# A graph network on one core: a first stage written out as one pipeline, and skip features added by TensorE

## Chip, core and metric

The kernel runs on one NeuronCore of a Trainium2 chip. The metric is the device time of one execution in microseconds (us), the median of several runs. Engines are named as in the profile: PE (TensorE), DVE (VectorE), ACT (ScalarE), POOL (GpSimd) and SP (SyncE, which here only issues DMAs).

## What is computed

6250 nodes with 128 features, 200000 edges sorted by destination. Two blocks, each with a residual. The change lies in the first block and in what prepares the edge lists; this is the part of the reference that it touches:

```python
h = jnp.maximum(_layernorm(x, axis=-1), 0.0)
# inside the first block
hn = _layer_norm(h, ln1_w, ln1_b)
h_skip = hn
ft = (hn @ W_att).reshape(n, H, DH)          # H = 10, DH = 13
...                                          # attention over the edges of each node, agg
out = jax.nn.elu(agg)
out = out.reshape(n, H * DH) @ hr_w + hr_b
out = out + h_skip
out = _layer_norm(out, in_w, in_b)
skip2 = out
out = jax.nn.elu(out @ w1 + b1)
out = jax.nn.elu(out @ w2 + b2)
return out + skip2
```

The second block is four graph convolutions over the same edges, done as dense products with a 6272 x 6272 matrix of edge counts.

## The kernel before, in words

Nodes are tiled by 128: 49 tiles, handled in 7 batches (`NB`) of 7 tiles (`BATCH`, 896 rows, `BW`). Edges are padded to 196 groups (`NG`) of 1024 (`GE`). The program is a row of stages with a barrier of all engines between them: `prelude` (the first stage), `attention`, `normalise`, `general_attention` (skipped for regular inputs), `node_update`, `convolutions`.

`prelude` does two unlike things. One is the node features (`node_features`): for each batch two layer norms (of x, rectified; then of that, with weight and bias), a transpose on PE, the projection by `W_att`, and two writes to DRAM, `hn_dram` (the normed features, needed again in the node update) and `ft_tab` (the projected ones, gathered by attention). DVE makes both norms' statistics and the whole second norm: four passes of 128x896, for mean (L570), scale (L577), weight (L582) and bias (L585). ACT makes the rectified first norm (L598) and copies the projection out (L611). A batch is a loop body, every buffer is single.

The other is the edge lists. The inputs `dst` and `src` are copied to padded lists in DRAM (L286 to L295), and when all fills are out (`pads_out`) the lists are read back in several layouts (L302 to L313): by partition of 1600 and of 1568 edges, the same shifted by one (`nxt_s`, to find where the order falls), and by group (`by_group`, 98 partitions). From them come: the counting (L368 on DVE compares every 56th destination with 1569 thresholds, L460 on PE sums that over partitions, 28 steps, with four buffers of `below` between them), the start of each strip of edges, the keys (L373 to L378, six passes), written to DRAM as `edge_key`, the sources turned by PE into `src_all` (L389), the group rows (`row_tab`), and the schedule. At the end POOL fetches keys by indirect DMA in 13 blocks (`BLOCKS`, four buffers, L272), PE turns each block (L490), DVE makes `key_cols` of it (L433) and ACT `low_cols` (L446), with one bank of PSUM between them. On every engine the node features stand first in the queue, then the counting, then keys, sources and rows, then the 13 blocks.

`node_update` is written out by hand as a pipeline over the 7 batches: in step i PE, ACT and DVE work on batches i-1, i and i+1. For batch i+1, PE turns the attention's output and projects it by `hr_w` in two parts (L1675, L1676: two matmuls for each of 7 tiles, each split in two by the fp32 type), DVE adds the normed features `hn`, loaded from DRAM, to the PSUM result (`add_skip`, L1517 and L1519), makes statistics, ACT normalises in place in `o` (L1603), DVE applies weight and bias (L1534, L1537) to give `s2`, PE turns `s2` for the feed-forward, and POOL adds `s2` to x (L1464).

Of the kernel before, what the change touches and what calls it, by code (L numbers as in the profile page):

```python
# [11 lines left out]
ds = bass.ds  # L12
# [58 lines left out]
def gnn_program(nc, t):  # L71
# [12 lines left out]
    hn_dram = dram("hn_dram", (NP, D), F32)  # L84

    top = ExitStack()
    with top:
# [25 lines left out]
        def ln_batch(nm, on):  # L113
# [7 lines left out]
                 agg_tab=agg_tab, edge_score=edge_score, adj=adj, hn_dram=hn_dram,  # L121
# [32 lines left out]
def rounds(engine, n, body):  # L154

    body(0, True)
    with engine.Fori(1, n) as i:
        body(i, False)


# [13 lines left out]
def prelude(nc, t, sb, pb, sem, g, ln_batch):  # L174

    dst_pad, src_pad, edge_key, ft_tab, row_tab, agg_tab = (g[k] for k in (
        "dst_pad", "src_pad", "edge_key", "ft_tab", "row_tab", "agg_tab"))
    x_sb, ident, ident_bf, ones, eps, irr_part, src_all, sched, shared, spots, key_cols, low_cols = (
        g[k] for k in ("x_sb", "ident", "ident_bf", "ones", "eps", "irr_part", "src_all", "sched", "shared", "spots",
                       "key_cols", "low_cols"))  # L180
    with ExitStack() as c:
        fill_no = sb("fill_no", [16, 512], I32, c)
        fill_zero = sb("fill_zero", [16, 512], I32, c)
        fill_neg = sb("fill_neg", [1, FRONT], I32, c)
        zero_f = sb("zero_f", [P, TAB // P // 5 * WA], F32, c)
        dst_p = sb("dst_p", [P, EXJ], I32, c)
        src_p = sb("src_p", [P, EXJ], I32, c)
        dst_s = sb("dst_s", [P, EJ], I32, c)
        strip_of = sb("strip_of", [P, EXJ], I32, c)
        keys = sb("keys", [P, EXJ, 2], F32, c)  # L190
        hi = key_cols[:].rearrange("p n a c -> p (n a c)")[:, 0:EXJ].bitcast(I32)
        kf = low_cols[:].rearrange("p n a c -> p (n a c)")[:, 0:EXJ]
        coarse = sb("coarse", [P, EJ // COARSE], F32, c)
        nxt_s = sb("nxt_s", [P, EJ], I32, c)
        falls = sb("falls", [P, EJ], F32, c)
        by_group = sb("by_group", [GH, 2, GE], I32, c)
        of_group_f = sb("of_group_f", [GH, 2, GE], F32, c)
# [19 lines left out]
        key_rows = sb("key_rows", [P, BELOW, SW, 2], F32, c)  # L217
        keys_ps = pb("keys_ps", [P, 512], F32, c)
        cnt_ps = pb("cnt_ps", [P, 512], F32, c)
        base_ps = pb("base_ps", [P, 512], F32, c)  # L220
        pool_const = sem("pool_const")
        filled = sem("filled")
        pads_out = sem("pads_out")
        lists_in = sem("lists_in")
        x_in = sem("x_in")
        keys_made = sem("keys_made")
        keys_out = sem("keys_out")
        below_made = sem("below_made")
        below_used = sem("below_used")
        falls_made = sem("falls_made")  # L230
        by_group_in = sem("by_group_in")
        by_group_f = sem("by_group_f")
        turned = sem("turned")
        turned_out = sem("turned_out")
        rows_made = sem("rows_made")
        rows_out = sem("rows_out")
        spots_made = sem("spots_made")
        spots_turned = sem("spots_turned")
        counts_summed = sem("counts_summed")
        starts_made = sem("starts_made")  # L240
        starts_turned = sem("starts_turned")
        start_at_made = sem("start_at_made")
        key_rows_in = [sem(f"key_rows_in{b}") for b in range(BLOCKS)]
        keys_turned = sem("keys_turned")
        key_cols_made = sem("key_cols_made")
        low_cols_made = sem("low_cols_made")
        dve_chain = sem("prelude_dve_chain")
        pool_chain = sem("prelude_pool_chain")
        features = node_features(nc, t, sb, pb, sem, g, ln_batch, c)
        block = c.enter_context(nc.Block())  # L250

        @block.gpsimd
        def _(pool):
            link = Chain(pool, pool_chain)
            nc.gpsimd.iota(row_no[:], [[0, 1]], base=0, channel_multiplier=1, allow_small_or_imprecise_dtypes=True)
# [1883 lines left out]
```

## Time and profile before

| | us |
|---|---|
| median of 3 runs | 5498.39 (5497.65 to 5499.48) |
| the profiled execution | 5488.85 |
| its span, first to last instruction | 5487.0 |

| engine | busy us | share of the span |
|---|---|---|
| PE | 4303.6 | 78% |
| DVE | 2203.1 | 40% |
| ACT | 1940.3 | 35% |
| POOL | 1511.9 | 28% |

How to read it: the shares are means over stages with different limits, so a change in one stage is judged from that stage. The profile names an instruction by engine, source line, output and inputs; a timeline line begins with the start and the length in us, `x7` merges seven alike, and the bracket at the end is the idle time of the engine before it and what ended that. The granted clock of PE is a share of 2.4 GHz: 0.5 is 1.2 GHz. `SPq` is the issue of a DMA on SP's queue.

### The profile page before, as it was taken

How to read it: one execution, taken by the hardware profiler on the slowest of the kernel's cores; microseconds unless marked ns; L12 is line 12 of the kernel's file. 1: busy time of each engine (PE TensorE's matmuls, PEld its weight loads, DVE VectorE, ACT ScalarE, POOL GpSimd, SP SyncE). 2: the span in 40 equal slices, each digit the busy share in tenths (PEclk: the TensorE clock that was granted, in tenths of full speed). 3: DMA queues.
4: the chain of work that ended last, by engine and by line, in shares of the span. 5: the costliest groups of instructions: out<-in, count | busy, mean ns of one | idle time of the engine just before them, and what ended most of it. 6: DMA issues, size and time to landing. Idle time of an engine off the chain costs nothing. (4 is left out here: it accounts for less than half of the span.)

```text
span 5487.0 us, 70225 instructions
## 1 busy us (share of the span) xinstructions
PE 4303.6 (78%) x21902; PEld 2477.3 (45%) x21902; DVE 2203.1 (40%) x3441; ACT 1940.3 (35%) x5106; POOL 1511.9 (28%) x1604
## 2 busy tenths in 40 slices
PE   4477777777677777777777777577999999999998
PEld 3244444444444444444444444344444444444444
DVE  6455555555555555555555555554101101101101
ACT  2354555544455554445554445355001001001000
POOL 0344444444444444444444444100000000000000
PEclk7566666666766666666666676688999999999999
DMA  4222222222222222222222222201565565565564
GB/s 146 73 68 61 61 61 65 63 61 61 61 61 61 64 63 61 62 61 61 62 64 62 61 62 61 69 17 50 196 203 176 196 202 177 195 202 177 194 202 155
DMA packets 470358, 556.57 MB, mean 101 GB/s; under 512 B 38252, under 2 KB 417285, under 8 KB 470113
## 3 DMA queue, kind: packets, MB, share of 16 engines
q1 hardware_dynamic: 390880, 369.08, 20.8%
q0 software_dynamic: 51168, 107.68, 8.9%
q10 hardware_dynamic: 28224, 78.69, 3.8%
q8 instruction: 51, 0.84, 0.1%
q14 instruction: 35, 0.28, 0.0%
HBM read 453.73 MB, written 103.18 MB: 101 GB/s over the span
## 5 line engine op out<-in xcount | busy, mean ns | idle before, releaser
L788 POOL DMA_INDIRECT fts<-ft_tab,src_all x1568 | 1481.1, 945 | 1794.9 <-DVE terms L862 1373.4
L2035 PE MATMUL cv_acc<-cv_cnt,cv_parts 128*128 128x512 bf16 (+1 forms) x7056 | 1429.5, 366 | 0.0
L2035 PEld LDWEIGHTS cv_acc<-cv_cnt,cv_parts 128*128 128x128 bf16 x7056 | 666.0, 98 | 764.1
L825 DVE TENSOR_TENSOR ohk<-iota_ps,key_cols 128x784 bf16<-128x784 f32 x784 | 720.7, 955 | 0.0
L1069 PE MATMUL most_ps<-signs,most 1*128 1x2 f32 x392 | 107.0, 340 | 764.3 <-DVE most L834 713.9
L1088 PE MATMUL agg_ps<-terms,oh 128*64 128x141 f32 x2744 | 671.3, 434 | 2.5 <-DVE terms L862 2.5
L1088 PEld LDWEIGHTS agg_ps<-terms,oh 128*64 128x64 f32 x2744 | 584.0, 222 | 53.1 <-issue 37.7
L918 ACT ACTIVATE dist_l<-lo_iota,low 128x128 bf16<-128x128 f16 x1960 | 593.4, 387 | 7.0
L1026 PE MATMUL adj_ps<-ohk,ohl 128*128 128x196 bf16 x3136 | 593.5, 336 | 0.0
L1888 DVE TENSOR_TENSOR cv_y<-cv_acc,cv_dis_row 128x512 f32<-128x512 f32 (+1 forms) x52 | 34.4, 661 | 1353.8 <-PE cv_acc L2035 1325.2
L834 DVE TENSOR_REDUCE most<-most_ps 1x1 f32<-1x128 f32 x196 | 54.6, 279 | 1262.8 <-DMA key_rows<-edge_key,start_at 1255.2
L1998 ACT ACTIVATE cv_sd<-cv_mv,eps 128x1 f32<-128x1 f32 x4 | 1.2, 294 | 1479.2 <-DVE cv_tmp L1940 1479.2
L965 ACT COPY res<-agg_ps 64x141 f32<-64x141 f32 x196 | 53.1, 271 | 1231.4 <-remote 1215.3
L1022 PE MATMUL adj_ps<-own,own_low 32*128 (+1 forms) x784 | 363.4, 463 | 131.3 <-DVE ohk L825 80.8
L970 ACT CAST strip<-adj_ps 128x392 bf16<-128x392 f32 x784 | 377.6, 482 | 243.5 <-PE adj_ps L1026 213.3
L1026 PEld LDWEIGHTS adj_ps<-ohk,ohl 128*128 128x128 bf16 x3136 | 311.6, 123 | 321.9 <-issue 308.4
L1069 PEld LDWEIGHTS most_ps<-signs,most 1*128 1x128 f32 x392 | 90.4, 285 | 811.8 <-DVE most L834 589.7
L839 DVE TENSOR_TENSOR prod<-ftd_ps,fts 128x780 f32<-128x780 f32 (+1 forms) x392 | 270.0, 689 | 288.1 <-PE ftd_ps L1048 250.2
L1048 PE MATMUL ftd_ps<-win,ohdT 64*128 64x130 f32 x3136 | 355.7, 353 | 0.8 <-DVE prod L839 0.8
L1048 PEld LDWEIGHTS ftd_ps<-win,ohdT 64*128 64x128 f32 x3136 | 257.2, 227 | 107.1 <-issue 106.2
L925 ACT ACTIVATE ohl<-dist_l 128x1280 bf16<-128x1280 bf16 x196 | 249.4, 1272 | 0.0
L875 DVE TENSOR_REDUCE score<-prod 128x80 f32<-128x1040 f32 x196 | 242.4, 1237 | 6.8
(261 smaller groups left out, 3444.7 us busy)
## 6 DMA issues: line engine op xcount, KB each, us to landing
cv_cnt<-adj SPq DMA_DIRECT2D x96, 2048.0 KB, 8.0
cv_cnt<-adj SPq DMA_DIRECT2D x48, 2176.0 KB, 8.3
adj<-strip ACTq DMA_DIRECT2D x196, 392.0 KB
fts<-ft_tab,src_all POOLq DMA_INDIRECT x1568
win<-ft_tab SPq DMA_DIRECT2D x196, 65.0 KB
agg_tab<-res SPq DMA_DIRECT2D x196, 35.2 KB
cv_cnt<-adj SPq DMA_DIRECT2D x8, 512.0 KB, 3.7
agg_tab<-zero_f SPq DMA_DIRECT2D x5, 705.0 KB
```

What stands on the lines that cost most here:

```text
L788: nc.gpsimd.indirect_dma_start(fts[u][:, k, :], None, ft_tab[:, :], bass.IndirectOffsetOnAxis(src_all[:, n, k:k + 1], 0)).then_inc(gathere ...
L825: nc.vector.tensor_tensor(ohk[:, k.s, at, :], key_no.unsqueeze(1).to_broadcast([P, QC, KEYS]), columns(key_cols, k)[:, at].unsqueeze(2).to ...
L839: nc.vector.tensor_tensor(by_half(prod[:]), ftd_ps[:, :, 0:n * HD].rearrange("p a (c f) -> p a c f", f=HD), by_half(fts[k.u][:]), ALU.mult ...
L875: nc.vector.tensor_reduce(score[:, k.s, 0:GC * H], prod[:].rearrange("p c (h d) -> p (c h) d", d=DH), AX.X, ALU.add).then_inc(score_done, 1)
L918: last = nc.scalar.activation(dist_l[:, n, :], lo_iota[:], ACT.Abs, bias=low[:, k.s, n:n + 1], scale=-1.0)
L925: nc.scalar.activation(ohl[:, k.s, LD:NA * SC, :], dist_l[:], ACT.Relu, bias=1.0, scale=-1.0).then_inc(ohl_done, 1)
L970: nc.scalar.copy(strip[:, k.s, :, QS * q:QS * (q + 1), :].rearrange("p t a d -> p a t d"), adj_ps[q % 2][:, 0:QS * KEYS].rearrange("p (a t ...
L1022: nc.tensor.matmul(adj_ps[q % 2][:, 0:QS * KEYS], own_low[:, P - SUB - SUB * k.u:2 * P - SUB - SUB * k.u], tile_of, start=True, stop=False)
L1026: last = nc.tensor.matmul(adj_ps[q % 2][:, a * KEYS:(a + 1) * KEYS], ohl[:, k.s, n, :], ohk[:, k.s, n, :], start=False, stop=(a == QS - 1 ...
L1048: last = nc.tensor.matmul(ftd_ps[:, half, m * HD:(m + 1) * HD], ohdT[at, k.u, (c0 + m) * P:(c0 + m + 1) * P], win[at, k.u, :], start=True, ...
L1088: nc.tensor.matmul(agg_ps[:, 0:WA], oh[:, k.u, col, half, :], terms[:, k.s, n, :], start=(n == 0), stop=False)
L2035: last = nc.tensor.matmul(a[:, 0:width], parts[:, r, b, :], cnt[q][:, 0:width // SUB, (b - b0) * SUB:(b - b0 + 1) * SUB], start=(b == 0 an ...
```

## The change

The first stage is rewritten as one pipeline, in which the node features and the list work share the cycles. There are no loops any more. In short:

- The lists are read from the inputs, in pieces whose row counts divide evenly (112 and the rest, 96 and the rest), on SP's queue (`dst`) and on ACT's (`src`, both lists by group, and the ends of groups and rows). The padded lists in DRAM are written later; nothing in this stage reads them. Only real edges get computed keys; the pad's keys are a constant written once.
- The cycles (`CYCLES`) run from -2 to 7; the first list of them below is that of DVE, the second that of ACT. Counting comes first on DVE and PE, then the starts and the keys; then come the node features, batch after batch, and in each cycle two of the 13 key blocks, with two banks of PSUM. Schedule, group rows and falls are made in cycles 3, 4 and 5.
- The second norm is done by ACT with scale and bias per partition (7 instructions a batch). Weight and bias are applied after the transpose, where a feature is a partition, in the copy from PSUM: half by DVE, half by ACT. Buffers are double or triple. The turned features go to DRAM (`hnT_dram`) in place of `hn_dram`.
- POOL fills the constants and converts both group layouts to floats. It no longer adds anything in the node update.
- In the node update the turned features are loaded, and PE adds them: a matmul of each tile with the identity, ahead of the projection in the same PSUM sum. Statistics and norm read PSUM. DVE adds `s2` to x.

```diff
+        def load_edges(engine, to, src, fill, done):
+            for r0, r1 in ((0, MANY), (MANY, FULL)):
+                engine.dma_start(to[r0:r1, :], src[r0 * EJ:r1 * EJ].rearrange("(p j) -> p j", j=EJ)).then_inc(done, 16)
...
+            pool.wait_ge(s["by_src_in"], 96)
+            nc.gpsimd.tensor_copy(src_f[:], by_src[:]).then_inc(s["src_f"], 1)
+            pool.wait_ge(s["by_dst_in"], 96)
+            nc.gpsimd.tensor_copy(dst_f[:], by_dst[:]).then_inc(s["dst_f"], 1)
...
+            sp.wait_ge(s["pool_const"], 1)
+            load_edges(sp, dst_s, t["dst"], fill_no, s["dst_in"])
...
+            sp.wait_ge(s["keys_made"], 1)
+            sp.dma_start(edge_key[0:EP, :].rearrange("(p j) k -> p (j k)", p=P),
+                         keys[:].rearrange("p j k -> p (j k)")).then_inc(s["keys_out"], 16)
...
+            counts()
+            for i in CYCLES:
+                if there(i):
+                    h_stats(i)
+                if there(i + 1):
+                    coefficients(i + 1, lnx, s["sd1"], s["h"], s["neg1"])
+                if there(i - 2):
+                    turned_features(i - 2)
+                if i == -1:
+                    edge_keys()
+                    fetch_places()
+                if there(i):
+                    coefficients(i, lnh, s["sd2"], s["u"], s["neg2"])
+                if i == 0:
+                    turned_sources()
+                if there(i + 2):
+                    x_stats(i + 2)
+                for b in pair(i):
+                    key_columns(b)
...
+            for i in CYCLES:
+                if there(i):
+                    root(i, lnh, s["var2"], s["neg2"], s["sd2"])
+                if there(i - 2):
+                    turned_features(i - 2)
+                if there(i + 1):
+                    rectified(i + 1)
+                if there(i):
+                    normal(i)
+                if there(i - 2):
+                    features_out(i - 2)
+                for b in pair(i):
+                    low_columns(b)
+                if there(i + 2):
+                    root(i + 2, lnx, s["var1"], s["neg1"], s["sd1"])
...
-            for i in range(NB):
-                pool.wait_ge(s["s2"], i + 1)
-                nc.gpsimd.tensor_tensor(x(i), x(i), s2[i % 2][:], ALU.add).then_inc(s["skipped"], 1)
...
-                nc.vector.tensor_tensor(o[:, 0:4, :], el_ps[:, 0, :].rearrange("p (b d) -> p b d", d=D),
-                                        hn[i % 2][:, 0:4, :], ALU.add)
...
+                stats(la, lambda b: block_of(el_ps, b)).then_inc(s["var1"], 1)
...
+                nc.vector.tensor_tensor(x(i), x(i), s2[:], ALU.add).then_inc(s["skipped"], 1)
...
+                    nc.tensor.matmul(at, hnT[i % 2][:, b, :], ident[:], start=True, stop=False)
+                    nc.tensor.matmul(at, elT[:, b, :], hr_w[:], start=False, stop=False)
                     last = nc.tensor.matmul(at, el3T[:], hr_3[:, b, :], start=False, stop=True)
```

## Rows read from the trace of the kernel before

**Rows 1.** The page, part 2: busy tenths of PE in 40 equal slices.

```profile
PE   4477777777677777777777777577999999999998
```

**Rows 2.** Busy time by stretch: length, PE, PEld, DVE, ACT, POOL, PE clock, DMA share, GB/s.

```profile
0.00:36.00 36.00, 1.69 (x8) 1.43 (x8) 15.33 (x70) 7.78 (x18) 2.74 (x11) 1.00 0.85 277
36.00:116.00 80.00, 34.74 (x142) 29.85 (x141) 61.84 (x220) 23.79 (x67) 0.00 (x0) 0.59 0.35 110
116.00:137.00 21.00, 20.75 (x116) 11.87 (x117) 18.18 (x28) 0.19 (x2) 0.00 (x0) 0.92 0.20 61
137.00:164.00 27.00, 9.25 (x45) 8.14 (x43) 24.66 (x33) 0.00 (x0) 0.43 (x1) 0.55 0.24 90
164.00:195.00 31.00, 13.88 (x52) 9.28 (x52) 5.41 (x16) 4.83 (x13) 12.12 (x14) 0.50 0.38 104
...
3606.00:3755.00 149.00, 119.98 (x408) 70.35 (x407) 92.01 (x249) 81.66 (x148) 8.33 (x4) 0.85 0.03 10
```

**Rows 3.** Timeline (start us, length us, instruction), SP's queue, first stage.

```profile
31.44 0.34 SPq L302 DMA_DIRECT2D dst_p<-dst_pad  x1
```

**Rows 4.** Timeline of one batch of node features, all engines.

```profile
63.41 1.44 DVE L498 BATCH_NORM_STATS2 nb_st<-nf_h 128x6 f32<-128x128 f32 x7
...
63.55 3.40 PE L628 MATMUL nf_ft_ps<-w_att,nf_hnT 128*128 128x130 f32 x14 [1.24 <-DVE nf_hnT L588]
...
65.00 0.58 DVE L502 BATCH_NORM_AGGREGATE nb_mv<-nb_st 128x2 f32<-128x6 f32 x7
...
65.61 1.09 DVE L570 TENSOR_TENSOR nf_u<-nf_h,nb_mv 128x896 f32<-128x896 f32 x1
...
67.06 1.04 ACT L611 COPY nf_ft<-nf_ft_ps 128x390 f32<-128x390 f32 x3 [5.85 <-PE nf_ft_ps L628]
...
70.65 2.80 ACT L598 ACTIVATE nf_h<-x_sb,na_nb,na_rs 128x128 f32 x7 [1.53 <-DVE na_nb L563]
...
74.58 0.69 DVE L587 COPY nf_hnT<-nf_T_ps 128x512 f32<-128x512 f32 x1 [1.85 <-PE nf_T_ps L622]
```

**Rows 5.** Timeline of counting, keys and turned sources, PE and DVE.

```profile
116.25 1.16 PE L460 MATMUL nf_ft_ps<-below,ones_bf 128*128 128x393 bf16 x3 [1.14 <-ACT nf_ft L611]
...
120.00 14.80 DVE L368 TENSOR_SCALAR below<-thr,coarse 128x1569 bf16<-128x1569 f16 x22 [0.28 <-PE cnt_ps L460]
...
141.19 1.82 DVE L376 SCALAR_TENSOR_TENSOR low_cols<-strip_of,dst_p 128x1600 f32<-128x1600 int32 x1
...
145.69 1.56 DVE L389 CAST src_all<-nf_T_ps 128x392 int32<-128x392 f32 x2
```

**Rows 6.** Timeline of the key fetch and the stage's end.

```profile
154.61 0.40 SPq L322 DMA_DIRECT2D edge_key<-keys  x1
...
163.57 1.13 POOL L272 DMA_INDIRECT key_rows<-edge_key,start_at  x1 [159.97 <-DMA edge_key<-keys]
...
193.54 0.22 ACT L446 COPY low_cols<-keys_ps 128x64 f32<-128x64 f32 x1 [1.10 <-DVE key_cols L433]
...
194.91 0.06 DVE L794 MEMSET score<- 128x1 f32 x1 [1.40 <-PEq L103]
```

**Rows 7.** Timeline of the node update: projections, skip adds and POOL's add.

```profile
3584.39 0.69 DVE L1517 TENSOR_TENSOR nu_o<-nu_el_ps,nu_hn 128x512 f32<-128x512 f32 x1 [3.22 <-PE nu_el_ps L1676]
...
3597.81 2.09 POOL L1464 TENSOR_TENSOR x_sb<-x_sb,nu_s 128x896 f32<-128x896 f32 x1 [24.73 <-DVE nu_s L1537]
...
3648.24 0.79 PE L1676 MATMUL nu_el_ps<-hr,nu_el3T 21*128 21x128 f32 x2
...
3649.17 0.68 DVE L1517 TENSOR_TENSOR nu_o<-nu_el_ps,nu_hn 128x512 f32<-128x512 f32 x1
...
3678.74 0.48 PE L1676 MATMUL nu_el_ps<-hr,nu_el3T 21*128 21x128 f32 x2
...
3680.90 0.68 DVE L1517 TENSOR_TENSOR nu_o<-nu_el_ps,nu_hn 128x512 f32<-128x512 f32 x1
```

**Rows 8.** Timeline of DVE at the start of attention.

```profile
241.43 0.97 DVE L839 TENSOR_TENSOR prod<-ftd_ps,fts 128x780 f32<-128x780 f32 x1 [32.87 <-DMA key_rows<-edge_key,start_at]
```

More of the change, by code:

```diff
@@ new lines, in _ @@
+            load_edges(act, src_s, t["src"], fill_zero, s["src_in"])
+            load_groups(act, by_src, t["src"], fill_zero, s["by_src_in"])
+            load_groups(act, by_dst, t["dst"], fill_no, s["by_dst_in"])
+            with nc.allow_non_contiguous_dma(reason="first and last destination of every group, and of every row"):
+                of_group = t["dst"][0:(NG - 1) * GE].rearrange("(g e) -> e g", e=GE)
+                act.dma_start(lasts[0:1, 0:NG - 1], of_group[GE - 1:GE, :]).then_inc(s["ends_in"], 16)
+                act.dma_start(bases[0:1, 0:NG - 1], of_group[0:1, :]).then_inc(s["ends_in"], 16)
+                act.dma_start(nxt[0:FULL - 1, :], t["dst"][EJ:FULL * EJ].rearrange("(p j) -> p j", j=EJ)[:, 0:1]
+                              ).then_inc(s["ends_in"], 16)
@@ new lines, in _, with root, rectified @@
+            act.wait_ge(s["filled"], 1)
+            def root(i, ln, var, used, done):
+                act.wait_ge(var, i + 1)
+                wait(act, used, i)
+                nc.scalar.activation(ln["sd"][:], ln["mv"][:, :, 1], ACT.Sqrt, bias=eps[:]).then_inc(done, 1)
+            def rectified(i):
+                act.wait_ge(s["neg1"], i + 1)
+                wait(act, s["hnT_ps"], i - 2)
+                for b in range(BATCH):
+                    last = nc.scalar.activation(h[i % 3][:, b, :], x_sb[:, i * BATCH + b, :], ACT.Relu,
+                                                bias=lnx["nb"][:, b:b + 1], scale=lnx["rs"][:, b:b + 1])
+                last.then_inc(s["h"], 1)
@@ new lines, in normal, with turned_features @@
+            def normal(i):
+                act.wait_ge(s["neg2"], i + 1)
+                for b in range(BATCH):
+                    last = nc.scalar.activation(h[i % 3][:, b, :], h[i % 3][:, b, :], ACT.Identity,
+                                                bias=lnh["nb"][:, b:b + 1], scale=lnh["rs"][:, b:b + 1])
+                last.then_inc(s["u"], 1)
+            def turned_features(i):
+                if not i:
+                    act.wait_ge(s["w_in"], 48)
+                act.wait_ge(s["hnT_ps"], i + 1)
+                wait(act, s["ft_done"], i - 1)
+                wait(act, hn_out[i % 2], 16 * (i // 2))
+                nc.scalar.activation(hnT[i % 2][:, 4:7, :].rearrange("f b p -> f (b p)"), T_ps[:, 1, 0:384], ACT.Identity,
+                                     bias=lnb[:], scale=lnw[:]).then_inc(s["hnT_b"], 1)
@@ new lines, in project @@
+            def project(i):
+                if not i:
+                    pe.wait_ge(s["w_in"], 48)
+                pe.wait_ge(s["hnT_a"], i + 1)
+                pe.wait_ge(s["hnT_b"], i + 1)
+                wait(pe, s["ft_sb"], i)
+                for b in range(BATCH):
+                    last = nc.tensor.matmul(ft_ps[:, b // 3, (b % 3) * HD:(b % 3 + 1) * HD], hnT[i % 2][:, b, :], w_att[:],
+                                            start=True, stop=True)
+                last.then_inc(s["ft_done"], 1)
@@ new lines, in turn_keys @@
+                last.then_inc(s["keys_turned"], 1)
+            for i in CYCLES:
+                for b in pair(i):
+                    turn_keys(b)
+                if there(i - 2):
+                    project(i - 2)
+                if there(i - 1):
+                    turn_features(i - 1)
+                if i == 2:
+                    pe.wait_ge(s["spots_made"], 1)
+                    nc.tensor.transpose(base_ps[0:5, 0:P], spot_cols[:], ident[:]).then_inc(s["spots_turned"], 1)
+            project(NB - 1)
```

737 lines of the change are left out of this document (353 added, 384 removed).

## The prediction

> **What bounds the kernel now.** I read the page's slices of busy time first: [rows 1]. PE is full only in the last third (the convolutions); the long middle at seven tenths is the attention loop. The change does not touch either of them. It rewrites the first stage and edits the node update, so I read those by stretches of time: [rows 2]. The stages are parted by barriers, so what a stage loses or gains arrives whole at the end. The first stage lasts from 0 to 194.9 us, where the first instruction of attention starts [rows 6], and it is a row of phases, one bound after another: lists and x come in (0 to 36, the DMA engines busy 0.85 of the time at 277 GB/s), then DVE makes the node features (36 to 116: 61.84 of 80 us busy, ACT only 23.79), then counting (116 to 137, PE 20.75 of 21), then keys and schedules on DVE (137 to 164: 24.66 of 27), then keys are fetched and turned (164 to 195: no engine over half). Five phases whose bounds are different engines stand behind each other: that is what can be overlapped.
>
> **First stage, part by part.**
>
> *Reads.* Before, the lists are padded in DRAM first and only read back at 31.44 us [rows 3]. After, both are read straight from the inputs, cut so that the big pieces have 112 or 96 rows. The first read waits for POOL's fills and one iota, 3 us. dst and src together are 1.6 MB, with the two group layouts 3.2 MB; at 277 GB/s [rows 2] that is 5.8 to 11.5 us, so dst is there at 9 to 15 us. I take 11. x (3.2 MB) and the zero fill (3.5 MB) come behind it, done by some 40 us, before the keys need the queue.
>
> *Counting* is now first. Its 28 steps are the same. PE alone sets them: 22 steps of DVE take 14.80 us, 0.67 each, and the first steps last 1.16 for three of four matmuls [rows 5], about double. The stretch was 21 us. Start 11, end 32.
>
> *DVE until the pipeline runs.* Statistics of a batch are 1.44+0.58 = 2.02 us [rows 4]. x statistics 2.0, then the four cuts to the first places (about 2) : 36. Coefficients 0.4. Keys: six passes over 1568 instead of 1600 columns, two of them 1.82 [rows 5], the four others about 1.0, 7.5 in all: 44. The 26 small matmuls that turn the places run beside the keys. Then places 0.3, x statistics 2.0, h statistics 2.0, coefficients 0.8, the turned sources 2 x 1.56 = 3.1 [rows 5], x statistics 2.0: 54. The conversion of the groups to floats is gone from DVE (2 x 1.2) and is POOL's, which has nothing else to do before the fetches.
>
> *Key fetch.* From the issue of the key write (154.61) to the first gather (163.57) are 9.0 us [rows 6]. Keys ready at 44 thus give gathers from 53, and columns from 57. That is early enough for cycle 1, which starts at 54. From there two of the 13 blocks ride in each cycle. Before, the 13 blocks cost 30 us by themselves (163.57 to 193.76); now they cost 0.8 us of ACT and 0.8 of DVE in a cycle.
>
> *The cycles.* A batch on ACT: rectify 2.80, normalise 2.80 (new: it takes over two DVE passes), features out 1.04 [rows 4], half of the turned copy about 0.5, two roots 0.6, low columns 0.8: 8.5 us. On DVE: 2 x 2.02, coefficients 0.8, the other half of the turned copy 0.69 [rows 4], key columns 0.8: 6.4 us. The passes that went (mean, scale, weight, bias, 1.09 each [rows 4]) are replaced by ACT's two per-partition operands and by lnw and lnb as scalars in the turned copy, which cost nothing more than that copy. PE has 3.4 for the projection [rows 4] and two sets of transposes that are each shorter, under 8 together. So ACT sets the pace with 8.6, except where DVE has extras: cycle 3 the schedule (2.4), cycle 4 the group rows (4.0), cycle 5 the falls (3.6), there 9 to 10.4. Cycles 1 to 7: 7.7+8.6+8.9+10.4+10.4+9+6.5 = 61.5, so 54+61.5 = 115.5. Tail: turned copy 0.7, projection 3.4, features out 1.0, write and landing 4.5: 125. The last DVE checks (some 6 us, an estimate: a part of the 24.66 us of [rows 2]) end beside it. Barrier as before, 193.76 to 194.91 [rows 6], 1.2: attention starts at 126 instead of 195. **Gain 69 us.** Bounds: 80 if ACT's pace holds in every cycle and dst lands at 9; 50 if lists land at 15, counting stays at the low clock for some steps and waits between the three engines add 1 us in each of ten steps.
>
> A rule that speaks against part of this: POOL now converts 98x2048 twice while DVE counts with a one-input 16-bit pass. No row here shows the two together; POOL's only wide operation, 2.09 us for 896 columns [rows 7], had DVE idle. In sentences of its own: the Trainium skill (SBUF — State Buffer, section "SBUF: two separate sides") says that DVE and GpSimd share a port pair, that it is locked for a whole instruction, and that the loser waits. From the row, a conversion could hold it for 2.09 x 2048/896 = 4.8 us; two of them would stop counting for up to 9.6 us, since PE has only four steps in hand.
>
> **Node update.** Gone: two DVE adds from PSUM per batch (0.68 + 0.55) and POOL's add (2.09). Added: seven projections of the turned skip by the identity on PE, and one DVE add of 1.09 from SBUF. That DVE add stands before the wait for the output exponential, where DVE idles some 5 us: nothing. The skip's load is fetched a batch ahead, in 3.5 KB rows: nothing, or up to 2 us less at the start of the stage.
> What counts is when statistics can start. A projection matmul pair takes 0.48 us at 2.4 GHz and 0.79 at 1.2 [rows 7], so seven more are 3.4 or 5.5 us. At batch 5's (3678.74) all are at the high clock and PE ends at 3679.22, DVE comes at 3680.90: 1.7 us slack. 3.4 - 1.7 - 1.2 (the saved adds) = +0.4. At 3648.24 the clock has fallen within the projection and PE ends 0.1 us before DVE comes: 5.5 - 0.1 - 1.2 = +4.2. In the first two batches DVE waits for PE anyway (3.22 us at 3584.39): +4.3 each. Behind the statistics stand root, table load, exponential and DVE again, so a delay goes through. Sum: 2 x 4.3 + 5 x (0.4 to 4.2, I take 2) = 19, less 1 for overlapping pairs and 2 for the load: **+16 us**, bounds +5 and +29.
>
> In sentences of its own: the Trainium skill (TensorE: Matmul & The Clock Gate, section "What's actually happening") has the clock released by activity, by which more matmuls would keep it up, and the addition would cost 5 rather than 16 us. The rows speak against: the fall comes within the row of small matmuls itself [rows 7].
>
> **Sum.** 5488.85 - 69 + 16 = 5436 for the profiled execution. Its time lies 9.5 us under the median 5498.39, so 5445 for the median.
>
> **Rivals.**
> A. The node update keeps its clock: +5, total -64: 5434. For it: 0.85 mean clock in its steady part [rows 2].
> B. Engines don't overlap as drawn: three engines pass each batch twice in both directions, and POOL's conversions stop the counting (9.6 us). The stage ends at 145 instead of 126, total -34: 5464. For it: ten steps, each with four hand-overs; against: nothing of ACT's 8.5 us waits for the same batch's own DVE pass.
> C. It does not do what it says: the first stage stays bound by DVE as before. Its DVE work was 125 us busy of 195; what is removed is 7 x 4 passes of 1.09 and 2.4, 33 us, so 92 remain, and with a start at 11 and half the old idle time (35) the stage takes 138: total -41: 5457.
> D. Slower. The stage is now written out in full, no loop. At the start of attention, also written out, DVE stands for 32.87 us [rows 8] while 32 gathers are issued, put down to a DMA that had long landed; PE and ACT stand as well. I take this to be a stall in the supply of instructions (argued, not shown). If the unrolled stage meets such a stall three times, 99 us, it eats the 69 and leaves +46 with the node update: 5544. It decides from two such stalls on. Against it: the node update is written out too and shows no such gap.
>
> **How the numbers follow.** Forecast 0.55 (5435 to 5455), A 0.15, B and C together 0.25, D 0.05. The range 5422 to 5478 goes from A with the gain at 80 (-75) to the gain of 50 with +29 (-21). Within 0.2% (11 us, what a measurement can tell from no change) only if B and the worst clock meet or one stall comes: 0.04. Faster 0.93, slower 0.03, as D's single-stall part falls into the others.
>
> **What the profile would show.** Counting starts at 9 to 15 us and ends at 29 to 37; the first gather of keys comes at 50 to 58; in cycles 2 to 6 ACT is over 80% busy with a pace of 8.6 to 10.4; attention's first memset stands at 120 to 135. In the node update the projection rows are 21 pairs a batch, DVE waits for PE before the first statistics, and the steady batch takes 31.7 to 36 us (now 31.7, from 3649.17 to 3680.90 [rows 7]). I am wrong if gaps of over 5 us without a releaser stand in the first stage, if DVE's counting passes get longer beside POOL's conversions, or if attention or the convolutions, which are not touched, move by over 5 us.

## The result: 82 us faster, below the forecast's range

| | before | after |
|---|---|---|
| median of 4 runs, us | 5498.93 (5497.65 to 5503.0) | 5416.68 (5394.82 to 5420.4) |
| ratio | | 0.984, 95% interval 0.9816 to 0.9863 |
| profiled execution, us (span) | 5488.85 (5487.0) | 5394.82 (5393.0) |

Forecast was 5445 with a range of 5422 to 5478. The sign and, for the first stage, most of the mechanism held; the time fell under the range, and the term for the node update had the wrong sign. The runs were made in several sessions on several chips. The kernel before took 5376 to 5503 us in some sessions (A below) and 4153 to 4164 us in others (B), so a ratio below always compares runs of one session. One chip number stands at both an A and a B session, so it is not shown that this is a fixed property of a chip.

The stages are parted by barriers, so both traces can be cut at the first instruction of each. Of the changed kernel (timeline: start, length, engine, line, what):

```profile
116.50 0.06 DVE L879 MEMSET score<- 128x1 f32 x1 [2.97 <-PEq L103]
...
3415.43 0.27 ACT L1050 COPY res<-agg_ps 64x141 f32<-64x141 f32 x1 [5.04 <-PE agg_ps L1186]
...
3443.38 0.35 SPq L1528 DMA_DIRECT2D hr_w<-in_L_gnn_hr_w  x1
...
3710.42 1.76 SPq L1864 DMA_DIRECT2D cv_W<-in_L_gnn_W  x4
```

Attention's first memset, its last result, the node update's first load and the convolutions' first. The same marks in the kernel before ([rows 6] has the first of them), and both kernels once more in a B session (runs e14 and e15 below), give the lengths in us:

| stage | before | after | | before, B | after, B | |
|---|---|---|---|---|---|---|
| first stage | 194.9 | 116.5 | -78.4 | 195.8 | 116.6 | -79.2 |
| attention | 3308.2 | 3298.9 | -9.3 | 1974.0 | 1973.9 | -0.1 |
| normalise | 27.5 | 28.0 | +0.5 | 27.6 | 27.9 | +0.4 |
| node update | 273.1 | 267.0 | -6.1 | 273.4 | 267.5 | -5.9 |
| convolutions | 1683.3 | 1682.6 | -0.7 | 1683.4 | 1684.3 | +0.9 |
| span | 5487.0 | 5393.0 | -94.0 | 4154.2 | 4070.2 | -84.0 |

So the change is worth 84 us: 78 in the first stage (forecast 69) and 6 in the node update (forecast 16 the other way). The first profiled pair shows 9 more, from attention, which the change does not touch.

The windows of the changed kernel by stage (length, then busy time of PE, PEld, DVE, ACT, POOL, PE clock, DMA share, GB/s), to lay beside [rows 2]; and the page's line of PE by slices, as [rows 1]:

```profile
0.00:36.50 36.50, 21.06 (x112) 11.27 (x112) 24.06 (x47) 0.00 (x0) 8.94 (x19) 1.00 0.93 231
36.50:50.70 14.20, 6.98 (x35) 6.64 (x34) 13.79 (x44) 5.00 (x12) 0.00 (x0) 0.57 0.61 230
50.70:99.60 48.90, 26.88 (x149) 24.55 (x149) 45.32 (x227) 44.32 (x123) 12.40 (x13) 0.70 0.53 172
99.60:116.50 16.90, 8.33 (x66) 7.38 (x64) 8.01 (x12) 7.54 (x21) 0.05 (x1) 0.92 0.74 231
```
```profile
PE   5677777777677777777777777587999999999998
```

Counting now runs while x is still arriving; from 50.7 to 99.6 DVE and ACT are both over 90% busy (45.32 and 44.32 of 48.90), where before DVE had 61.84 of 80 with ACT at 23.79. That is the overlap drawn in the prediction.

### The profile page after: what moved, and what is told of

The parts are those of the page before. It is cut to its first block and busy times, and to the rows that moved or that the text cites. A ratio compares the mean times of both kernels' runs of the same rounds, so it can differ in the third digit from the quotient of the medians.

```text
span 5393.0 us, 70281 instructions
## 1 busy us (share of the span) xinstructions
PE 4263.2 (79%) x22000; PEld 2463.4 (46%) x22000; DVE 2169.0 (40%) x3401; ACT 1957.6 (36%) x5162; POOL 1501.6 (28%) x1605
```

## Experiments on the first stage

**One piece instead of an even split (e6).** Each list is read with one DMA for its full rows: 127 rows for `dst` and for `src`, 98 and 97 for the halves of the group layouts. (The expectation says 125 rows; 127 is right.)

```diff
-            for r0, r1 in ((0, MANY), (MANY, FULL)):
+            for r0, r1 in ((0, FULL),):
...
-                for g0, g1 in ((0, GMANY), (GMANY, GH - half)):
+                for g0, g1 in ((0, GH - half),):
```

> The changed kernel with each list read in one piece of 125 rows (of 98 and 97 for the groups) instead of 112+13 (96+2). Theory that the even split matters: dst, ready for DVE's first list pass at 13.6 us now, comes 3 us or more later, counting and the stage's end move with it (attention starts at 119.5 or later). Rival: all 16 DMA engines are busy with the 3.2 MB either way, dst comes at 13.6 +- 1 and attention starts at 116.5 +- 1.

Measured: 5415.39 us against 5420.94 before, ratio 1.0015 (0.9983 to 1.0047). Nearly the whole gain is gone: attention starts at 190.8 us, 74.3 later than in the changed kernel. Timeline of DVE and of SP's queue, and the window:

```profile
67.06 0.18 DVE L423 CAST coarse<-dst_s 128x28 f32<-128x28 int32 x1 [63.47 <-DMA dst_s<-fill_no]
```
```profile
4.64 26.85 SPq L263 DMA_DIRECT2D dst_s<-fill_no  x1
```
```profile
4.00:31.00 27.00, 0.00 (x0) 0.00 (x0) 0.00 (x0) 0.00 (x0) 1.41 (x7) 1.00 0.06 25
```

DVE waits 63.47 us for the list (10.00 in the changed kernel). From 4 to 31 us the DMA share is 0.06, one engine of 16, and 25 GB/s move; in the changed kernel it is 0.98 and 231 GB/s from 4 us until the list is there. The queue's next issues stand behind the read, one of them 26.85 us. The Trainium skill (DMA: Bandwidth & Descriptors, section "Why a DMA increments its semaphore by 16 and not by 1") has the number of DMA engines as the largest one up to 16 that divides the slowest dimension of both sides, so 1 for 127 rows and 16 for 112. This trace agrees, with 0.06 against 0.98. The list is 53.5 us late, and that is not all of the 74: issues on ACT's queue stand as well (one of them 31.86 us), and the keys' write goes out at 118.30 instead of 46.21 us, 72 later. The prediction's first term took 277 GB/s for granted. It held only because of the split: what I passed over in half a sentence was worth 74 us. The expectation had its sign, not its size (3 us or more).

**Key blocks last (e7).** The blocks of `turn_keys`, `key_columns` and `low_columns` follow the last batch.

```diff
-                for b in pair(i):
-                    turn_keys(b)
...
             project(NB - 1)
+            for b in range(BLOCKS):
+                turn_keys(b)
```

> The changed kernel with the 13 key blocks after the last batch instead of two in each cycle, as in the kernel before. Theory (the overlap itself gives a good part of the gain): 13 blocks by themselves take 13 x 1.2 = 16 us with two banks (30 us before with one), the cycles lose 7 x 0.5 us of ACT, DVE's last checks follow instead of lying beside; the first stage ends 12 to 18 us later, at 129 to 135. Rival: the blocks fit beside the last checks and the cycles are shorter without them: +5 or less.

Attention starts at 132.1, 15.6 us later; ratio 0.9893 (0.9823 to 0.9963). This is inside the theory's 12 to 18, so the overlap of the key blocks with the features is worth 15.6 us.

**Second norm on VectorE (e11).** Two wide passes in place of ACT's seven instructions.

```diff
+                    link(nc.vector.tensor_tensor(h[i % 3][:], h[i % 3][:], lnh["rs"][:].unsqueeze(2).to_broadcast(wide),
+                                                 ALU.mult))
+                    nc.vector.tensor_tensor(h[i % 3][:], h[i % 3][:], lnh["nb"][:].unsqueeze(2).to_broadcast(wide),
+                                            ALU.add).then_inc(s["u"], 1)
...
-                if there(i):
-                    normal(i)
```

> The changed kernel with the second norm made by VectorE in two passes of 128x896 (scale, shift) instead of ACT's seven instructions with scale and bias per partition. Theory: in cycles 3 to 6 VectorE sets the pace already (10.1, 9.8, 7.6 and 5.7 us, with the schedule, the group rows and the falls in them), so 2.2 us more in each of 7 batches come out nearly whole there and by some 0.5 in the others: the stage ends 9 to 15 us later, at 126 to 132. Rival: ACT's relief of 2.7 us a batch pays for it, and the stage ends within 4 us of 116.5.

Attention starts at 128.2, 11.7 us later (ratio 0.9831, 0.9814 to 0.9847, against 0.9797 for the changed kernel in another B session). Two passes of 1.09 us in each of seven batches are 15.3 us; three quarters of that come out. ACT's relief does not pay for it, as in the middle cycles both engines are over 90% busy and DVE has the extras.

**The conversions on GpSimd (e8, e13).** e8 adds one wait ahead of the first conversion, e13 moves both to ACT.

```diff
             pool.wait_ge(s["by_src_in"], 96)
+            pool.wait_ge(s["counts_summed"], 1)
```
```diff
-            nc.gpsimd.tensor_copy(src_f[:], by_src[:]).then_inc(s["src_f"], 1)
...
+            nc.scalar.copy(src_f[:], by_src[:]).then_inc(s["src_f"], 1)
```

> The changed kernel with GpSimd's first conversion held until the counting is done. Theory: the conversions (1.9 and 2.2 us) disturb VectorE's counting passes a little, 22 steps of 16.0 us against 14.8 in the kernel before: counting ends 1 to 1.5 us earlier, and so does the stage (115 to 115.5), since the sources are turned 8 us later. Rival: the passes are longer for another reason (DMAs), and counting ends at 36.5 as now.

> The changed kernel with the two conversions of the group layouts (98x2048, int to float) on ACT, which has nothing to do before 36 us, instead of GpSimd. Theory: GpSimd's conversion and VectorE's counting pass exclude each other, so that one pass beside each takes up to 2.25 us instead of 0.63; on ACT they don't, all 28 passes take 0.61 to 0.64, the gap of 0.8 us in TensorE's counting is gone, counting and the stage end 0.8 to 1.5 us earlier (attention starts at 115.0 to 116). Rival: the long passes come from the DMAs that write SBUF at the same time; then they stay, and nothing moves.

The 28 counting passes of DVE (shortest, median and longest in ns), of the changed kernel and of e13:

```profile
L427 DVE TENSOR_SCALAR below<-thr,coarse x28: 614/624/2251, 13.8 to 33.9; 128x1569 bf16<-128x1569 f16 x28
```
```profile
L423 DVE TENSOR_SCALAR below<-thr,coarse x28: 618/631/635, 14.6 to 33.1; 128x1569 bf16<-128x1569 f16 x28
```

Timeline of the changed kernel: the conversions, and PE where it ran out of counting steps:

```profile
18.19 1.89 POOL L294 CAST src_f<-by_src 98x2048 f32<-98x2048 int32 x1 [12.55 <-DMA by_src<-fill_zero]
22.21 2.21 POOL L296 CAST dst_f<-by_dst 98x2048 f32<-98x2048 int32 x1 [2.12 <-DMA by_dst<-fill_no]
```
```profile
24.89 0.68 PE L647 MATMUL nf_ft_ps<-below,ones_bf 128*128 128x393 bf16 x3 [0.78 <-DVE below L427]
```

Two of the 28 passes are long, one beside each conversion: 2.01 and 2.25 us instead of 0.63. None is when ACT converts, with the same DMAs running: the rival is out. In e8 the conversions lie elsewhere and hold something else (timelines of POOL and DVE):

```profile
36.82 1.90 POOL L295 CAST src_f<-by_src 98x2048 f32<-98x2048 int32 x1 [31.16 <-PE cnt_ps L648]
38.65 1.90 POOL L297 CAST dst_f<-by_dst 98x2048 f32<-98x2048 int32 x1
```
```profile
38.83 1.74 DVE L400 SCALAR_TENSOR_TENSOR na_nb<-na_mv,na_rs 128x7 f32<-128x7 f32 x1
```

A pass over 7 columns, 0.17 us otherwise, ends at 40.57, when the second conversion ends (40.55). The Trainium skill's rule of the shared port pair (SBUF — State Buffer, section "SBUF: two separate sides"), which the prediction cites, holds for the mechanism: exclusive, for a whole instruction. Its price here is small: four steps of `below` in hand cover most of it. e13's counting ends 0.75 us earlier and stays ahead by that much, until the last but one projection runs at the low clock (3.37 instead of 1.80 us): attention starts at 117.4, no gain (4072.78 us; 4072.01 in e15, the changed kernel in the same session). In e8 it starts at 118.7. Both theories (a start at 115 to 116) missed. e8's median, 5314.97 us, is 106 under that of the kernel before in its session (ratio 0.9838, 0.9768 to 0.9908), but its profile has attention at 3203.3 us where e7's has 3230.3 and e6's 3263.0; that cannot be put down to the edit.

**The last checks moved into gaps (e17).** On top of e13.

```diff
+                if i == 6:
+                    oddities()
+                if i == 7:
+                    judged()
             turned_features(NB - 1)
-            oddities()
+            last_checks()
```

> The changed kernel with the conversions on ACT, and with VectorE's last checks (3.3 of 5.3 us of them) moved from the end of the stage into cycles 6 and 7, where VectorE stands 1.9, 1.4 and 2.5 us. Theory: VectorE ends 3 us earlier, at 110.4, and the stage then ends with the last write of the projected features (issued at 111): attention starts at 114.5 to 116, 1 to 2 us before the changed kernel. Rival: the write's landing already sets the end, and the moved checks delay the last turned copy by 0.2 to 0.5 us: 116.5 to 117.5, no gain.

The rival came out: DVE ends at 112.8 instead of 115.0, but attention starts at 118.2, against 117.9 in the changed kernel of the same session (e18). In both the last write of `ft_tab` is issued at 112.5. In e18 it lands 3.7 us later, behind DVE's end, so by these numbers the stage ends with that landing. Of the 12.6 us between 5386.03 and 5398.58, the profiles have 10.3 in attention (3275.2 and 3285.5). No version here beats the changed kernel by what could be told.

## Experiments on the node update

**The node update alone (e2).** Kernel before, with the new `node_update`; its first stage writes the turned features.

> The kernel before with the node update of the changed one alone (the old first stage writes its turned features, with weight and bias, instead of the straight ones). Theory (the 7 more pairs keep the clock up, and they cost little at the high clock): the node update takes 265 to 269 us as against 273.1 before, all projection pairs from the second batch on at 0.48 us or less, the first stage as before within 2 us; about 5493 in all, -6. Rival, the prediction's term: 7 more pairs of 0.48 to 0.79 us each, exposed: 273 + 16 = 289, about 5514.

Ratio 0.9985 (0.9976 to 0.9994), 7 us by the medians. The node update takes 267.9 us, and the old first stage 192.5, 2.4 less than before. So the new node update alone saves 5 us, and the price of +16 is refuted.

**GpSimd adds again (e4).**

```diff
-                nc.vector.tensor_tensor(x(i), x(i), s2[:], ALU.add).then_inc(s["skipped"], 1)
+                nc.gpsimd.tensor_tensor(x(i), x(i), s2[i % 2][:], ALU.add).then_inc(s["skipped"], 1)
```

> The changed kernel with the add of s2 to x on GpSimd again, as before (s2 has two buffers again); the skip stays on TensorE. Theory: the add lay beside other work on either engine, so the node update stays at 267 +- 1.5 and the total within the run-to-run spread. Rival (the GpSimd add held VectorE up before, and moving it is what saved 6 us): DVE's passes next to it get longer, and the node update goes up by 3 to 6 us.

267.0 us: the engine of this add has no part in the gain, and GpSimd's add held nothing up before. Ratio 0.9844 (0.9829 to 0.9859).

**Without the skip matmuls (e3), with two sets of them (e12).** e3 leaves the skip features out of the sum, e12 adds them twice.

```diff
-                    nc.tensor.matmul(at, hnT[i % 2][:, b, :], ident[:], start=True, stop=False)
```
```diff
                     nc.tensor.matmul(at, hnT[i % 2][:, b, :], ident[:], start=True, stop=False)
+                    nc.tensor.matmul(at, hnT[i % 2][:, b, :], ident[:], start=False, stop=False)
```

> The changed kernel without the seven matmuls of the skip features (they are left out of the sum). Theory that they keep the clock up: 14 pairs are 1.5 us shorter in a batch than 21, but the clock falls again within the projection or the feed-forward's first quarters (pairs of 0.79, quarters of 3.3 us instead of 1.77) in several batches, and the node update stays between 263 and 268 us (now 267.0). Rival (what was saved is DVE's adds from PSUM, the clock follows something else): the clock stays up, and the node update falls by 7 x 1.5 = 10.8 to 256.

> The changed kernel with the skip matmul of each tile done twice in the node update (the skip features count double in the sum). Theory: one such pair costs 0.22 us, 1.5 in a batch, and lay just beside VectorE's work (its end 0.2 us ahead of VectorE's statistics), so a second set of seven comes out nearly whole: 1.3 us in each of five batches and 1.5 to 3 in the first two, the node update goes from 267 to 276 +- 2. Rival, the price of the prediction (0.48 us a pair, 3.4 a batch): 267 + 22 = 289 or more.

The stage takes 256.2 and 280.6 us (267.0 with one set). The ratios, 0.983 in both, are of sessions A (e3) and B (e12). One tile of the changed kernel, the middle of a batch (timeline of PE; each row is one pair), then a tile of the kernel before:

```profile
3584.11 0.49 PE L1749 MATMUL nu_el_ps<-ident,nu_hnT 128*128 128x128 f32 x2
3584.44 0.39 PE L1750 MATMUL nu_el_ps<-hr_w,nu_elT 128*128 128x128 f32 x2
3584.75 0.48 PE L1751 MATMUL nu_el_ps<-hr,nu_el3T 21*128 21x128 f32 x2
3585.17 0.49 PE L1749 MATMUL nu_el_ps<-ident,nu_hnT 128*128 128x128 f32 x2
```
```profile
3677.49 0.49 PE L1675 MATMUL nu_el_ps<-hr_w,nu_elT 128*128 128x128 f32 x2
3677.91 0.48 PE L1676 MATMUL nu_el_ps<-hr,nu_el3T 21*128 21x128 f32 x2
3678.32 0.49 PE L1675 MATMUL nu_el_ps<-hr_w,nu_elT 128*128 128x128 f32 x2
```

From tile to tile it is 1.06 us now and was 0.83, the pairs 0.42 apart. The added pair costs 0.22 us, 1.5 a batch, not the 0.48 printed, and e12's tile is 0.22 longer again. At the low clock, in the first batch, it costs 0.43 (3.0 for seven: 13.19 us instead of 10.20). Next come DVE of the changed kernel, PE at the same place in e3, and PE of the changed kernel:

```profile
3588.50 1.15 DVE L1565 SCALAR_TENSOR_TENSOR nu_uT<-nu_odd_ps,nu_b,nu_exF 128x896 f32<-128x896 f32 x1
3589.57 1.47 DVE L1578 BATCH_NORM_STATS2 ua_st<-nu_el_ps 128x6 f32<-128x128 f32 x7
```
```profile
3583.28 3.23 PE L1761 MATMUL nu_even_ps<-nu_s2T,nu_w 128*128 128x448 f32 x4
3586.30 1.94 PE L1761 MATMUL nu_odd_ps<-nu_s2T,nu_w 128*128 128x448 f32 x4
```
```profile
3589.39 1.77 PE L1762 MATMUL nu_even_ps<-nu_s2T,nu_w 128*128 128x448 f32 x4
3590.99 1.67 PE L1762 MATMUL nu_odd_ps<-nu_s2T,nu_w 128*128 128x448 f32 x4
```

The statistics start right behind DVE's own last pass, with no idle: the projection is done 0.2 us earlier (PE goes on at 3589.39). Without the skip matmuls (second fence) PE's clock has fallen by the next quarter of the feed-forward, 3.23 us; with them (third) it is up, 1.77. This is so in each batch from the second on, so the theory that they hold the clock is right. But a comparison with e3 shows that this is worth nothing in the middle of the stage. From one feed-forward's second half to the next a batch takes 30.58 us with them and without (3567.35 to 3597.93; e3: 3562.64 to 3593.22), so PE does not set it there. e3's 10.8 us come from the ends: 3.4 up to the first such place, 2.4 and 0.4 in the next two batches, 1.2 in the last but one, and 3.3 from there to the end. The rival's number came out, but not by its mechanism (7 x 1.5). The second set in e12 is exposed, 13.6 us, more than the 9 of the theory: 12.3 of them are the length of the added pairs (3.0 in the first projection, at the low clock, and 1.56 in each of the six others).

## Experiments on attention and the spread

**The same kernels again (e1, e14, e15, e18).**

> The changed kernel unchanged, to see where its times differ from run to run (5394.8 to 5420.4 so far, against 5497.7 to 5503.0 of the kernel before). Theory: the attention loop, which the change does not touch, makes all of the spread: the first stage ends at 116.5 +- 1.5, the node update (first DMA issue of the stage to the first of the convolutions) is 267 +- 2, the convolutions 1682.6 +- 1, and attention (first memset to last result copy) is anywhere from 3299 to 3325, with the granted clock of the loop following it. Rival: the new first stage itself varies (its DMAs), then its end moves by 5 us or more from one profile to the next.

> The kernel before unchanged, for a trace on the same chip as the next. Theory: first stage 193 to 195, node update 273 +- 1, convolutions 1683 +- 1; attention as long as in the next run within the spread of this chip (1 us on a fast chip, up to 50 on a slow one).

> The changed kernel unchanged. Theory: first stage 116.5 to 118, node update 267 +- 1, convolutions 1683 +- 1, so 78 + 6 = 84 less than the run before it plus what attention happens to differ. Rival: the change itself makes attention shorter (9 us in the first pair), then it does so here too.

> The changed kernel unchanged, on this chip. First stage 116.5 to 117.5, node update 267 +- 1, convolutions 1683 +- 1; attention 1974 on a fast chip, 3200 to 3310 on a slow one.

e1: 5399.55 against 5486.68, ratio 0.9843 (0.9829 to 0.9856); first stage, attention, node update and convolutions 117.1, 3302.0, 267.1 and 1683.8. In e1 to e4, all of one session, attention took 3302.0, 3308.5, 3299.9 and 3309.4 us; the convolutions differed by 1.5, the new first stage by 0.4. e15 against e14: 4072.01 and 4155.96, -84, the attentions 1973.9 and 1974.0. e18: 117.9, 3285.5, 267.9. So the 9 us of the first pair are within what attention differs from profile to profile, and e1's theory that the changed kernel's spread of 25 us is attention's fits all of these; the kernel before has the same spread (5467 to 5493 in e1's session). How the loop looks in an A session (the changed kernel's first run) and in a B session (e15), the same code; timelines of GpSimd, then of DVE at the start of the stage:

```profile
1008.85 0.94 POOL L873 DMA_INDIRECT fts<-ft_tab,src_all  x1 [7.24 <-DVE terms L947]
```
```profile
962.61 0.94 POOL L873 DMA_INDIRECT fts<-ft_tab,src_all  x1 [0.30 <-issue]
```
```profile
162.61 0.97 DVE L924 TENSOR_TENSOR prod<-ftd_ps,fts 128x780 f32<-128x780 f32 x1 [32.45 <-remote]
```
```profile
132.44 0.97 DVE L924 TENSOR_TENSOR prod<-ftd_ps,fts 128x780 f32<-128x780 f32 x1 [2.18 <-PE ftd_ps L1133]
```

In B (second and fourth) GpSimd issues gathers without a break, 8 x 1.25 = 10 us a group. In A it stands some 7.2 us in each group, as it waits for DVE, and in the same group DVE had stood for 6.55 us, ACT for 6.27 and PE for 4.15, from the middle of the gathers to 2 us behind the last. The stall at the start of attention, 32.87 us in [rows 8] and 32.45 here, is not there in B either.

**Unused matmuls in the gap (e5, e9, e10, e16).** PE stands 4 us in each group in an A session, and its clock falls. e5 puts 24 pairs of 128 columns there, e9 and e16 six bf16 ones of 512 (the edit shown), e10 twelve.

```diff
+                if k.exists() and two.exists():
+                    pe.wait_ge(strip_done, 4 * k.n)
+                    for _ in range(6):
+                        nc.tensor.matmul(adj_ps[1][:, 0:4 * P].rearrange("p (a b) -> p a b", a=4), ident_bf[:],
+                                         ident_bf[:].unsqueeze(1).to_broadcast([P, 4, P]), start=True, stop=True)
```

> The changed kernel with 24 matmuls of the identity by itself (fp32, 128 columns, 0.13 us each at the high clock), result unused, put into the attention loop where TensorE stands for 4 to 4.5 us in each group of 17 us (ahead of the matmul that spreads the highest score). It tells what sets the attention loop's pace and its spread. Theory: the loop's time follows the granted clock, whose fall costs about 2 us in a group; with TensorE busy in the gap the clock stays at 1.0 and a group takes 14.5 to 15.5 instead of 16.9 us: attention 2850 to 3050 instead of 3300, and its steps all alike. Rival: the clock does not matter for the loop (gathers set it), then nothing moves; or the 24 run at the low clock, take 6 us and push each group by 2: attention 3650.

> The changed kernel with 6 unused bf16 matmuls of 128x512 (0.21 us each at 2.4 GHz, 0.43 at 1.2) ahead of the matmul that spreads the highest score, where TensorE stands for 4 to 4.5 us in each group of attention. The 24 small pairs of an earlier run kept the clock at 0.87 on average but filled 8 us, gaps between them included, and a group took 20.1 us; behind them the rest of a group's TensorE work took 5.9 instead of 11.3 us. Theory: the clock sets the pace; 6 wide ones take 1.3 to 2.6 us, fit the gap, and hold the clock for a part of the group: 14.5 to 16.5 us a group, attention 2900 to 3200. Rival: too little to hold the clock, groups stay at 16.9, attention as without (3200 to 3310).

> The same with 12 wide matmuls: 2.6 us at the high clock, 5.1 at the low one. Theory: fits the gap at the high clock, holds it all through: group 14 to 15 us, attention 2750 to 2950, and the groups all alike, granted clock of the loop over 0.9. Rival: it starts at the low clock, overruns the gap by 1 us in each group and stays there: 17.5 to 18 us a group, attention 3450.

> The kernel with 6 unused wide matmuls in each group of attention, again, in case this chip is one on which the loop takes 3200 to 3300 us. Theory now: on such a chip the engines stand for 6 to 7 us in every group until GpSimd's gathers are all issued, all of them at once, so it is the issue of instructions and not the clock; the wide matmuls change attention by less than 100 us. Rival: the clock falls in this gap and costs 2 us a group; with it held, attention is 300 us or more shorter. On a chip where the loop takes 1975 us nothing changes either way.

e5, in an A session: 6114.88 us, ratio 1.131 (1.124 to 1.138), worse than its theory and than its rival. One group of it: GpSimd's first and last gather, then PE ahead of the gap and in it:

```profile
993.22 0.95 POOL L873 DMA_INDIRECT fts<-ft_tab,src_all  x1 [10.75 <-DVE terms L947]
1001.99 0.95 POOL L873 DMA_INDIRECT fts<-ft_tab,src_all  x1 [0.30 <-issue]
```
```profile
996.97 0.94 PE L1133 MATMUL ftd_ps<-win,ohdT 64*128 64x130 f32 x12
998.55 0.81 PE L1197 MATMUL adj_ps<-ident 128*128 128x128 f32 x5
1000.39 0.36 PE L1197 MATMUL adj_ps<-ident 128*128 128x128 f32 x1 [1.04 <-issue]
1001.81 0.27 PE L1197 MATMUL adj_ps<-ident 128*128 128x128 f32 x1 [1.05 <-issue]
1003.23 0.37 PE L1197 MATMUL adj_ps<-ident 128*128 128x128 f32 x1 [1.15 <-issue]
1003.97 7.34 PE L1197 MATMUL adj_ps<-ident 128*128 128x128 f32 x40 [0.37 <-issue]
```

For the first 6 us of the gathers PE runs at its usual pace. Then, until a microsecond behind the last one, it gets one small matmul through in 1.4 us with nothing but issue ahead of it, and afterwards 40 run in 7.34. The clock was held (0.83 in this group, against 0.60 in one of the changed kernel), but a group takes 20.5 us instead of 16.9. So in A sessions PE, which waits for no engine and no data there, gets its instructions late in the second half of the gathers. That much the rows show. That they are late because the gathers go out, and that DVE's and ACT's idle time has the same cause, is argued from the same timing: no run changes the gathers. e9, e10 and e16 fell into B sessions: 0.9803 (0.9786 to 0.9819), 1.0133 (1.0116 to 1.0150) and 0.9797 (0.978 to 0.9813); six change nothing (attention 1974.4 and 1974.6), twelve cost 137 us. Whether six help in an A session was not tried, and what sets A and B apart stays open.

## The prediction, point by point

- *dst at 11, counting done at 32.* 13.6 and 36.5. Late by 2.6, then 1.9 more for PE's first steps at the low clock and the conversions.
- *Conversions up to 4.8 us each.* 1.89 and 2.21: the price scaled from a two-input add was double. The mechanism stood, and one of my signs of being wrong with it (counting passes do get longer), but the cost was 0.75 us of counting.
- *Keys at 44, gathers at 53, cycle 1 at 54.* 46.2, 53.35 (7.1 us after the write's issue, not 9.0) and 56.3.
- *Cycles 1 to 7 in 61.5 us.* They took 51.5, the term of this stage that was mis-sized. From one batch's second statistics to the next's they are 6.8, 5.9, 10.1, 9.8, 7.6, 5.7 and 5.7 us, against 7.7, 8.6, 8.9, 10.4, 10.4, 9 and 6.5. Rows of ACT, then of DVE:

```profile
65.89 2.79 ACT L588 ACTIVATE nf_h<-x_sb,na_nb,na_rs 128x128 f32<-128x128 f32 x7
68.58 2.79 ACT L595 ACTIVATE nf_h<-nf_h,nb_nb,nb_rs 128x128 f32<-128x128 f32 x7
71.27 1.01 ACT L612 COPY nf_ft<-nf_ft_ps 128x390 f32<-128x390 f32 x3
...
73.64 2.81 ACT L588 ACTIVATE nf_h<-x_sb,na_nb,na_rs 128x128 f32<-128x128 f32 x7
...
91.74 2.79 ACT L588 ACTIVATE nf_h<-x_sb,na_nb,na_rs 128x128 f32<-128x128 f32 x7
```
```profile
82.39 1.45 DVE L380 BATCH_NORM_STATS2 na_st<-x_sb 128x6 f32<-128x128 f32 x7
...
88.89 1.44 DVE L389 BATCH_NORM_STATS2 nb_st<-nf_h 128x6 f32<-128x128 f32 x7
...
96.46 1.44 DVE L389 BATCH_NORM_STATS2 nb_st<-nf_h 128x6 f32<-128x128 f32 x7
```

  ACT's pace was priced by adding printed lengths, 8.5 us; from rectify to rectify it is 7.75, as each row starts 0.1 us before the one ahead of it ends. That gives about 2 of the 10 us, in cycles 1 to 3. Six more lie in cycles 5 and 6, which start at 88.89 and 96.46 and were priced almost as full ones. But work that runs ahead has ended by then: DVE's last x statistics (82.39) lie in cycle 4 and ACT's last rectify (91.74) in cycle 5, so cycle 5 has 2.0 us less of DVE's work and cycle 6 has 2.8 less of ACT's.
- *Tail to 126.* The tail was 8.7 us instead of 10.5, attention at 116.5. In all 78.4 of a foreseen 69, inside its bounds of 50 to 80, but near the upper one without what that asked for: the list at 9 us, and ACT's pace of 8.5 in every cycle.
- *Node update +16, bounds +5 to +29.* The failed step, 22 us off and outside its bounds: -6. It priced the added pairs at their printed lengths, 3.4 us a batch, or 5.5 where the clock had fallen [rows 7], and set 1.7 us of slack against that at one batch, next to none at the others. The added pair costs 1.5 us a batch, which fits the 1.7 us of slack that I had read off myself; only in the first batch, at the low clock, do the seven cost 3.0. What was left over is the gain of DVE's two adds from PSUM, 1.2 us a batch: a batch of [rows 7] whose projection kept the high clock went from 31.73 to 30.58 us. That these adds are the cause is read from these rows; no run takes them out alone. (e4 rules out GpSimd's add as the cause, and e3, which is faster still, the skip matmuls.) The sign "a steady batch takes 31.7 to 36 us" failed with it.
- *Rival A and the clock.* The Trainium skill's rule (TensorE: Matmul & The Clock Gate, section "What's actually happening") that activity releases the clock was right against my reading of [rows 7]. In the kernel before three of the seven projections, of 14 pairs each, fell to 1.2 GHz on their way and took 7.36, 7.32 and 7.28 us, where three others took 5.79. With 21 pairs none falls from the second batch on, and all six take 7.35. So where the clock used to fall the added pairs cost PE nothing, and such a batch (the one after that of 31.73 us) went from 33.08 to 30.58 us, 1.3 more than the other. But e3 keeps the clock in most of its projections with 14 pairs as well, so the pairs are not all that decides it. A's 5434 rested on the same price of the pairs and was too high as well.
- *Rivals B, C, D* did not occur: no gap without a releaser over 5 us stands in the first stage, and nothing like the stall of [rows 8] was met there.
- *Attention moves by over 5 us: then I am wrong.* It moved by 9.3, within what it differs in the repeats; in a B session it moved by 0.1. A single profiled pair can't bear a threshold of 5 us in a stage of 3300.

With the right terms the sum would have been 5488.85 - 78 - 6 = 5405 for the profiled execution and 5414 for the median, where 5416.68 was measured.

## To carry to other kernels

Price a row of like instructions by the distance of their starts, not by printed lengths, let an addition first fill the slack you read before any of it counts as exposed, and ask of each step of a pipeline which work has already run out in it. For a DMA, look at how its outermost dimension divides over the 16 engines before a bandwidth is assumed: 127 rows ran on one. Cut both traces at the barriers and repeat both kernels before a difference in an untouched stage is explained.

## What the chip showed that was not expected

- One and the same program took 4153 to 4164 us in some sessions and 5376 to 5503 in others, all of the difference in the loop that gathers through GpSimd (1974.0 and 3308.2 us).
- A read of 127 rows ran on one DMA engine of 16 (share 0.06, 25 GB/s), and later issues on its queue stood behind it for up to 31.86 us.
- A third matmul pair in a sum cost 0.22 us where each of two had cost 0.42, at the same clock and shape as one of them.
- In e8 a VectorE pass of 7 columns with two SBUF inputs was held 1.57 us by GpSimd's conversion, while the three one-input passes from PSUM beside the same conversions kept their 0.5 us each.
